# Self-attention and feed-forward in one program, the first up products between the last tiles

## The reference

```python
x = x + xattn(layernorm(x), ctx_768, ...)
# self-attention: 16 heads of 32, 32 rows in a sequence
qkv = layernorm(x) @ w_attn
scores = q @ k.T / sqrt(32) + causal - log1p(softplus(decay) * log1p(dist))
x = x + (softmax(scores) @ v) @ w_proj
# feed-forward: 512 -> 2048 -> 512
h = round8(layernorm(x) @ w1 + b1)         # to multiples of 2^-8
h = round8(piecewise_linear_gelu(h))       # 33 breakpoints on [-4, 4]
x = x + round8(h @ w2 + b2)
```

## Time and profile before

| | us |
|---|---|
| median of 3 runs | 1637.65 (1637.59 to 1638.66) |
| profiled execution: first to last instruction | 1631.5 |
| median run less that span | 6.15 |
| TensorE busy | 1582.6 |
| self-attention's first product to its last | 992.94 to 1247.58 |
| feed-forward's first product | 1249.76 |
| granted TensorE clock over the span | 0.993 of 2.4 GHz |

### The profile page before, as it was taken

The page is one execution under the profiler, slowest core; times in us unless marked ns, Lnnn a source line. Parts: engine busy times, 40 slices in busy tenths (PEclk is TensorE's granted clock), DMA queues, the critical chain, the costliest instruction groups (busy, mean ns, idle before and its releaser), DMA issues. The chain is left out here.

```text
span 1631.5 us, 30117 instructions
## 1 busy us (share of the span) xinstructions
PE 1582.6 (97%) x11126; PEld 1382.6 (85%) x11126; DVE 1229.8 (75%) x2404; ACT 1033.8 (63%) x2050; POOL 771.8 (47%) x722
## 2 busy tenths in 40 slices
PE   7999999999999999999999999999998999999998
PEld 5878899998999999899999778988886777878886
DVE  5548888877887888878887784666666988788886
ACT  3347777777777777777786422445446766666665
POOL 2316546364554546555453241334435545555554
PEclk9999999999999999999999999999998999999999
DMA  7983434444343443534353862011132221010010
GB/s 232 276 244 95 135 91 113 121 112 134 90 123 111 108 134 95 140 95 110 114 144 83 290 220 72 21 60 62 64 111 79 71 71 53 26 52 20 7 52 26
DMA packets 173826, 173.63 MB, mean 106 GB/s; under 512 B 80944, under 2 KB 138352, under 8 KB 173680
## 3 DMA queue, kind: packets, MB, share of 16 engines
q1 hardware_dynamic: 173680, 171.71, 36.2%
HBM read 133.91 MB, written 37.75 MB: 105 GB/s over the span
## 5 line engine op out<-in xcount | busy, mean ns | idle before, releaser
L75 PE MATMUL p_bank_score<-p_ctxt,p_qo 128*128 128x256 f32 x2304 | 304.5, 286 | 1.0 <-ACT p_probs L998 0.6
L75 PEld LDWEIGHTS p_bank_score<-p_ctxt,p_qo 128*128 128x128 f32 x2304 | 288.1, 191 | 6.1 <-issue 2.4
L75 PE MATMUL p_bank_mix<-p_probt,p_ctx 128*128 128x512 f32 x1152 | 292.1, 398 | 0.5
L75 PEld LDWEIGHTS p_bank_mix<-p_probt,p_ctx 128*128 128x128 f32 x1152 | 207.5, 189 | 41.8 <-issue 3.8
L2017 PE MATMUL p_bank_down<-p_w,p_ht 128*128 128x512 f32 x768 | 188.2, 393 | 7.0 <-DVE p_raw L2091 4.9
L1990 POOL TENSOR_TENSOR p_pieces<-p_pieces 128x512 f32<-128x512 f32 x64 | 112.3, 1755 | 159.2 <-ACT p_pieces L2057 159.2
L1201 DVE SCALAR_TENSOR_TENSOR p_qo<-p_bank_mix,p_odd,p_qo 128x512 fp32r<-128x512 f32 x192 | 143.8, 749 | 57.2 <-ACT p_qo L1012 49.5
L704 POOL TENSOR_TENSOR p_ctx<-p_ctx_in,p_ctx 128x768 fp32r<-128x768 f32 x64 | 118.3, 1849 | 131.6 <-ACT p_ctx L987 131.2
L2017 PEld LDWEIGHTS p_bank_down<-p_w,p_ht 128*128 128x128 f32 x768 | 143.8, 188 | 42.1 <-DVE p_raw L2091 6.5
L1012 ACT ACTIVATE p_qo<-p_bank_mix,p_odd 128x512 fp32r<-128x512 f32 x192 | 132.2, 689 | 67.8 <-PE p_bank_mix L75 67.4
L998 ACT ACTIVATE p_probs<-p_bank_score,p_small 128x257 f32<-128x257 f32 x256 | 121.3, 475 | 58.9 <-DVE p_small L1182 54.4
(11 more groups left out here) (276 smaller groups left out, 3631.9 us busy)
## 6 DMA issues: line engine op xcount, KB each, us to landing
p_blocks_in<-in_ctx_dram SPq DMA_DIRECT2D x256, 96.0 KB, 2.4
p_ctx_in<-in_ctx_dram SPq DMA_DIRECT2D x64, 384.0 KB, 3.1
q<-p_ctx SPq DMA_DIRECT2D x64, 256.0 KB, 3.6
p_odd_in<-in_ctx_dram SPq DMA_DIRECT2D x64, 192.0 KB, 3.5
p_x<-in_x_dram SPq DMA_DIRECT2D x32, 256.0 KB, 4.2
p_quad<-q SPq DMA_DIRECT2D x32, 256.0 KB, 3.8
p_probt<-q SPq DMA_DIRECT2D x32, 256.0 KB, 4.1
p_o_in<-o SPq DMA_DIRECT2D x8, 1024.0 KB, 7.1
```

Source lines behind the costliest of these rows:

```text
L75: made = e.matmul(out, lhsT, rhs, start=n == 0, stop=n == last)
```

## The change

The two blocks become one. Each engine runs its list of self-attention and then that of the feed-forward with no meeting between them, and parts of the feed-forward's lists (`following`) are called from within self-attention's.

- TensorE: up products 0 to 4 lie between the scores, mixes and projections of the last two tiles; up 5 precedes the first down product.
- The activation chain of product 0, the rounding of products 1 to 3 and the Abs and Relu of product 0 lie in self-attention's lists. What waits for them stays in order.
- The next stage's first four row tiles are turned in t = 8 to 11, as a second turn of each tile, and no longer in t = 12 to 15. Rows are scaled in place in four buffers, and a row's buffer is loaded again once it is turned.
- The late pieces: four in t = 14 and four in t = 15 (two on VectorE and two on GpSimd in each), the last four in n = 1 to 4 of the feed-forward.
- The last four projections use the turning bank. LayerNorm's moments for the feed-forward are prepared in three parts: 0 to 3, 4 to 11 (now in t = 14), 12 to 15 (n = 17 to 20).
- The bias is loaded at the start of self-attention, behind four row loads where there were three ahead of the decay's.

```diff
 def sync(e, following):
+    for p in range(4):
+        load_row(p)
     e.dma_start(dec[:], decay_raw[None, :].to_broadcast([P, HS])).then_inc(decay_in, DMA)
...
+    e.wait_ge(norm.steps, 14)
+    following.load_bias(e)
...
+        if t == LAST:
+            late_is_split(e, 2)
+            for k in range(2):
+                following.load_block(e, k)
 LAST = NT - 2 ; PAIRED = NT - 8
-LATE_EVEN = {NT - 2: ((0,), ()), NT - 1: ((2,), ()), NT: ((4, 6), (8, 10))}
-LATE_ODD = {NT - 2: ((), (1,)), NT - 1: ((), (3,)), NT: ((5, 7), (9, 11))}
+LATE_HI = {LAST: range(4), LAST + 1: range(4, 8)}
+LATE_EVEN = {LAST: (0, 2), LAST + 1: (4, 6)}
+LATE_ODD = {LAST: (1, 3), LAST + 1: (5, 7)}
 def tensor(e, following):
+    def turn_own(i):
+        j = i - PAIRED - 4
+        if j > 0:
+            e.wait_ge(after.norm.lo, j)
+        norm.turn(e, i)
+    def turn_next(j):
+        e.wait_ge(norm.lo, PAIRED + 4 + j + 1)
+        after.norm.turn(e, j)
+    for t in range(LAST):
+        scores(t)
+        project_slice("q", t + 2, 0, queried)
+        project_slice("k", t + 2, C, keyed)
+        if t >= 1:
+            mix(t - 1)
+        if t + 4 < NT:
+            turn_own(t + 4)
+        if t >= 2:
+            project(t - 2)
+        if PAIRED <= t < PAIRED + after.early:
+            turn_next(t - PAIRED)
+        project_values(t + 2)
+    scores(LAST)
+    project(LAST - 2)
+    following.up(e, 0)
+    mix(LAST - 1)
+    following.up(e, 1)
+    scores(LAST + 1)
+    project(LAST - 1)
+    mix(LAST)
+    following.up(e, 2)
+    following.up(e, 3)
+    mix(LAST + 1)
+    project(LAST)
+    following.up(e, 4)
+    project(LAST + 1)
 def scalar(e, following):        # t = 15, then behind the loop
+    if t == NT - 1:
+        following.fold(e, 0)      # Gelu's table, Abs, Relu
+following.gelus(e, 0)            # behind the cuts of tile 15
 def vector(e, following):        # in t
     e.wait_ge(scored, NB * (t + 1))   # mask, max
+    if t == NT - 1:
+        following.rounded_up(e, 0)
...                              # sum, reciprocal
+    if t == NT - 1:
+        following.rounded_up(e, 1)
...                              # transposition
+    if t == LAST:
+        after.norm.finish(e, 1)
+    if t + 4 < NT:
+        norm.low(e, t + 4, *ahead.place(t + 4))
+    if t >= 2:
+        sums(t - 2)
+    if PAIRED <= t < PAIRED + after.early:
+        after.norm.low(e, t - PAIRED, after.zt, (t - PAIRED) * P)
+    for k in late_blocks(LATE_EVEN, t):
+        low_late_even(e, k)
+# behind the loop
+following.rounded_up(e, 2)
+following.snap(e, 0)
+following.rest_of(e, 0)
+following.rounded_up(e, 3)
+sums(LAST)
+following.combine(e, 0)
+sums(LAST + 1)
 # feed-forward
 def tensor(e):
-    for n in range(NT + LAG):
-        if n < NT:
-            up(n)
-        if n >= LAG:
-            down(n - LAG)
+    for n in range(LAG, NT + LAG):
+        if n == LAG:
+            up(e, n + 1)
+        if n > LAG + 1 and n < NT:
+            up(e, n)
+        down(n - LAG)
 def scalar(e):
+    for n in range(1, NT + LAG):      # fold(n), gelus(n), high_block(n), high half of h
+        if n <= 4:
+            attention.late_high(e, 7 + n)
+        if n == KF + 2:
+            norm.root(e, 2)
 def vector(e):
+    for n in range(1, NT + LAG):      # from n = 4 on rounded_up(n)
+        if n == KF + 1:
+            norm.guard(e, 2)
+        if n == KF + 4:
+            norm.finish(e, 2)
+        if n in (2, 4):
+            attention.low_late_even(e, 6 + n)
```

More of the change, by code:

```diff
@@ L1396, in self_attention @@
         y_stats = room.sb("y_stats", [P, 6])
-        norm.banks = after.norm.banks = room.banks("turn", 1)
-        after.norm.z = norm.z
+        turn = room.banks("turn", 1)
+        norm.banks = turn
         mm = room.banks("mm", 3)
@@ L1444, in bank_of @@
         def bank_of(kind, n):
-            return mm[use_at[kind, n] % 3]
+            return mm[use_at[kind, n] % 3] if (kind, n) in use_at else turn[0]
         def bank_is_free(e, kind, n):
+            if (kind, n) not in use_at:
+                if n == LAST - 2:
+                    e.wait_ge(after.norm.lo, after.early)
+                else:
+                    e.wait_ge(added, n)
+                return
             at = use_at[kind, n]
@@ L1478, in sync @@
                 load_y(i)
+            e.wait_ge(norm.steps, 14)
+            following.load_bias(e)
             for t in range(NT):
-                if t + 7 < NT + after.early:
-                    load_x(t + 7)
+                for p in range(4, len(rows)):
+                    if row_step(p - 4) == t:
+                        load_row(p)
                 if t + 2 in WEIGHTS:
@@ L1803, in vector @@
             e.wait_ge(made, 7)
[L1804 removed]
+            for t in range(NT):
                 if t == SEEN:
@@ L1862, in feed_forward, with __init__ @@
+class FeedForward:
+    def __init__(self, begun, programs):
+        (self.load_bias, self.load_block, self.make_constants, self.up, self.fold, self.gelus, self.rounded_up,
+         self.snap, self.rest_of, self.combine) = begun
+        self.programs = programs
+def feed_forward(nc, ahead, attention, spare, w1, x2_dram, w_1, b_1, w_2, b_2, out_rows):
     G = 512
@@ new lines, in make_constants, with up @@
+        def make_constants(e):
+            e.memset(plus, MAGIC).then_inc(consts, 1)
+            e.memset(minus, -MAGIC).then_inc(consts, 1)
+            e.memset(last, LAST).then_inc(consts, 1)
+            e.memset(base, -SNAP - LAST).then_inc(consts, 1)
+            e.memset(quarter, STEP - SNAP - LAST).then_inc(consts, 1)
+        def up(e, n):
+            g, f = divmod(n, KF)
+            zt = zts[g % 2]
+            if f == 0:
+                e.wait_ge(norm.lo, NR * (g + 1))
+            if n == 0:
+                e.wait_ge(ahead.w_lo, KT)
+            if g == 0 and f >= KT and f % KT == 0:
+                attention.late_is_split(e, f // KT)
+            if n >= 3:
+                e.wait_ge(rounded, n - 2)
+            else:
+                attention.bank_is_done(e, n)
+            accumulate(e, b_up[n % 3], [t for k in range(KT) for t in three(
+                lambda s, k=k: first_weights(s, k, f),
+                lambda s, k=k: zt[:, s, k, :])]).then_inc(upped, 1)
@@ new lines, in fold @@
+        def fold(e, n):
+            m, a, w = (x[n % SETS] for x in (m_, a_, w_))
+            if n == 0:
+                e.wait_ge(consts, 5)
+                e.activation(scratch, quarter, ACT.Gelu).then_inc(ready, 1)
+            e.wait_ge(rounded, n + 1)
+            if n >= SETS:
+                e.wait_ge(downed, NR * (n - SETS + 1))
+            e.activation(a[:], m[:], ACT.Abs, bias=minus).then_inc(absed, 1)
+            e.wait_ge(absed, n + 1)
+            e.activation(w[:], a[:], ACT.Relu, bias=last, scale=-1.0).then_inc(left, 1)
```

479 lines of the change are left out of this document (236 added, 243 removed).

## The result

The changed kernel takes 1644.74 us in the median of five runs (1642.48 to 1645.9), the kernel before on the same chip 1637.65 (1635.88 to 1641.58). The ratio is 1.0047, with a 95% interval of 1.0033 to 1.0062: 5.4 to 10.2 us more. I had forecast 1639.6 and "no change" as the likeliest. The time lies 0.3 under the upper end of my range (1633.5 to 1645.0) and outside the sum's own, 1636.0 to 1641.9, and the sign is slower.

What follows compares the result with a forecast made beforehand. TensorE, busy 97% of the span, was taken as the bound. Terms 0.82 + 6.12 + 0.43 - 5.4 = +2.0 us on 1637.65 gave 1639.6; range 1633.5 to 1645.0, the sum's own 1636.0 to 1641.9.

Steps and rivals of the forecast that it cites:

- Behind it both orders are the same, and the lead stays as the chain's: After product 3 of the feed-forward: its 5.4 us of earliness against the kernel before lasts to the end.
- -5.4 for the end: From the scores of tile 14 on: product 3's low half of h at 60.7 instead of 66.14, 5.4 us earlier.
- the 17.9 from product 0 to 3: Low half of h, product 0 to product 3: 15.92 us before, 17.9 with late pieces 8 and 10 on VectorE.
- product 0's low half at 42.8: Start of the low half of h for product 0, 42.8 us after the scores of tile 14; before, 50.22.
- late pieces 8 and 10: Two weight pieces on VectorE between products 0 and 3: 0.65 to 1.64 us each, taken as 1.0.
- The third moment part: LayerNorm work in feed-forward group 1: costs nothing, as low halves are ready some 5 us early; without that, up to 4.
- The second turn: Tiles 8 to 11: it waits for VectorE's low half, stalling TensorE 1.53 us four times, +6.12; lowest price 1.39 each.
- The fourth row load ahead of the decay's: Start of self-attention: the extra load's issue on SyncE delays the decay by 0.43 us, at least 0.
- (1): Rival, faster: the second turn doesn't hold TensorE, only occupancies remain; -4.1, 1633.5 us; chance 0.17.
- (2): Rival, slower: TensorE's clock falls at the stalls in tiles 8 to 11; one +3.7, four +8.8 us; chance 0.2.
- (3): Rival, slower end: product 0's activation chain starts another 2 us later than 42.8; +4.0, 1641.6 us; chance 0.2.
- product 3's low half at 60 to 62: Sign in the feed-forward: prediction wrong if product 3's low half of h isn't 60 to 62 us after tile 14's scores.

Runs made afterwards that it cites:

- run 11: Run 10's kernel with late weight pieces 8 to 11 moved out of the steps of products 2 to 5 into engines' idle time: 1631.29 us, ratio 0.9968.
- run 10: Changed kernel with the edits of run 3, run 5, run 7 and run 9, and the decay's load ahead of the fourth row load: 1636.12 us, ratio 0.9991.
- run 9: Changed kernel with VectorE's snap and rest of product 1 ahead of combining product 0 and the sums of tile 15: ratio 1.0029 to the kernel before.
- run 5: Changed kernel with the third moment part on GpSimd except its reciprocal: ratio 1.0040 to the kernel before.
- run 6: Changed kernel with the low halves of late pieces 8 and 10 on GpSimd in place of VectorE: ratio 1.0059 to the kernel before.
- run 1: Kernel before with 64 bytes of padding ahead of the feed-forward's row, activation and h buffers: ratio 1.0003.
- run 2: Changed kernel with the gap ahead of the feed-forward's buffers raised from 80 to 96 words: ratio 1.0036 to the kernel before.
- run 7: Changed kernel with 192 bytes more ahead of the feed-forward's buffers (gap of 128 words): ratio 1.0047 to the kernel before.
- run 3: Changed kernel with the second turn of tiles 8 to 11 behind the value products: ratio 1.0006 to the kernel before.
- run 8: Changed kernel with the edits of run 3, run 5, run 6 and run 7, and the decay's load ahead of the fourth row load: 1637.76 us, ratio 1.0003.
- run 4: Kernel before with the feed-forward's PSUM banks in the changed kernel's order (turning bank first, then up, then down): ratio 0.9997.

## Why the prediction was wrong

**The failed step** is "Behind it both orders are the same, and the lead stays as the chain's", with the size of the lead that went into it. The sum booked -5.4 for the end; the end gave -0.42. The first step to fail is the one right ahead of it, the 17.9 from product 0 to 3. The missing 5.0 are four leaks, in the order in which they come:

- *The step to product 3*, 1.4. The start of the chain was right: product 0's low half at 42.8 forecast, 42.55 measured (1269.89 less 1227.34). But from there to product 3 I took 17.9, "late pieces 8 and 10 ... at 0.65 to 1.64 each; I take 1.0", and it was 19.54: 1.36 of the lead, after the 0.25 that product 0 came sooner. The 2.0 booked for the pieces was about right, as all four together cost 2.1 (run 11 against run 10), VectorE's own two at 1.77 and 1.79. What I put at nothing is the snap of product 1: I had the sums of tile 15 stand ahead of it and charged them to no step, and they cost 1.0 (run 9). The other 0.5 is in the step to product 1, which even in run 11 takes 5.39 for 4.85; no run says why. A further 0.2 goes by product 4.
- *The third moment part*, 1.2, booked as "nothing" because low halves were ready 5 us before their down products. That slack is TensorE's, within the group. VectorE has none: it is the chain across the next group boundary, so the 1.2 from product 16 to 19 (3.77 to 2.61) were lost for good, 1.0 of them in the one step that run 5 shortened. My "up to 4" for a missing cover was too high.
- *The place of the buffers*, in no term: 1.3 us of the last group, where TensorE sets the end (the profiles of runs 5, 6 and 9; 1.5 and 1.6 in those of runs 1 and 2, none in run 7's). The profile of before couldn't show it; the diff, which re-ordered the allocations, could have raised the question.
- *A fall of the clock in this one profile*, 1.0. From product 48 to 63 the lead falls by 2.3, where runs 5, 6 and 9, with the same buffers, lose 1.3. In this profile and in run 3's, which loses 2.2, the granted clock fell beside product 34, in those of runs 5, 6 and 9 beside product 18. The same 8 us of the changed kernel and of run 9, columns as in the earlier trace rows, the clock 0.79 and 1.00:

```profile
1466.00:1474.00 8.00, 6.20 (x19) 4.31 (x19) 6.86 (x11) 4.12 (x6) 0.77 (x2) 0.79 0.49 175
1466.00:1474.00 8.00, 7.58 (x32) 5.53 (x31) 6.73 (x12) 4.93 (x8) 1.45 (x1) 1.00 0.61 217
```

  TensorE is later from there on: product 57's down product starts 7.9 after its low half has ended, in runs 5, 6 and 9 7.3. Run 7 has that fall too and loses nothing, so it costs only together with the slower pace. That the fall is the cause rests on two profiles against three; no run was made for it.

So 5.4 less 1.4, 0.2, 1.2, 1.3 and 1.0 leaves 0.3, and 0.42 was measured; 0.1 came back between product 19 and 48. One more chance is in the number that I started from: product 0's 50.22 of the kernel before is 49.4 and 49.3 in runs 1 and 4, so 0.9 of every lead here is that profile's.

**Right, by its numbers.** The second turn waits each time. Counted as I counted it, from 2.89 after the projection's start, the wait is 1.44 where I had 1.53 (1190.35 and 1194.68; the profile's own idle time, which begins at the modelled end, is 1.29, under my floor of 1.39). Tiles 8 to 11 came to +7.77 for the forecast 7.76 (run 3 splits it into 6.0 of wait and 1.76 of turns); that it fits to the hundredth is luck. Tiles 12 and 13 gave back 0.80 for 0.82. The first down product came at 44.34 for "43 to 44", the wait before mix 14 was 1.97 for 2.4, and the two late pieces of tile 14 took 3.41 for 3.28. The Trainium skill, SBUF — State Buffer, section "Who interferes with whom", would have made that 3.9, by the prediction's estimate; what it says of who blocks fits all the same: a piece that started beside a running GpSimd operation took 1.77 (changed kernel, 1274.31), and one that started 0.02 ahead of it 0.66, while GpSimd's took 1.66 for 1.16 (run 11, 1253.01).

**A term too small.** The fourth row load ahead of the decay's: 0.43 booked as its issue. The wait for the decay grew from 3.55 to 4.5, and the stage to the scores of tile 0 by 0.93. All seven profiles with the fourth row load ahead wait 4.1 to 5.1; with the decay's load ahead of it again it was 3.6 to 3.9 (runs 8, 10 and 11), and 3.3 to 4.0 with the kernel before's own order.

**The rivals.** (1), that the turn doesn't hold TensorE, is excluded by the waits. (2), a fall of the clock at those waits, didn't happen: the clock is 1.00, and tiles 8 to 11 take 68.01 to 68.05 in all six profiles that keep the paired turn. (3) had the right sign with the wrong place, and is too small, +4.0 where the median rose by 7.1: the chain starts in time and then falls behind. That the time lies inside the range is luck: its upper end was made of two falls of the clock in tiles 8 to 11, and none came. My test "product 3's low half at 60 to 62" just failed at 62.10, and that was the first sign.

## What to carry to other kernels

A lead is worth what is left of it at the next place where its engine is the bound. Follow the engine that carries it through every stage to the end, and charge each operation that the change puts on that engine, however short and however well covered for the others. Work that must go near a chain through several engines belongs in a gap in which all of them wait, ahead of the chain (run 11: 5.2 us under the kernel before to run 10's 1.5 by the ratios, 4.4 to 3.1 by the profiles), not between its steps on whichever engine looks idle. And a wait for a buffer can be hidden by putting independent work between the two uses (run 3: 6.0 us for one moved line).

## What the runs showed of the hardware

The pace of a dense stretch of products depends on where its two SBUF operands lie: 227 ns a matmul of 512 columns with h and the turned rows at 128 modulo 256 bytes (two places of h, 162944 and 157056), as the other operand, and 231 to 233 ns at 192 and at 0 (the kernel before and run 7; the changed kernel, run 1 and run 2). PSUM's order changes nothing (run 4). It is the pair that counts: the same rows at 128 took 234 ns with the quarter of w1 at 224. That equal places modulo 256 are what makes a pair fast is only my reading, and it isn't clean: rows and weights both at 224 took 231 in the third group of the kernel before. The Trainium skill, TensorE: Matmul & The Clock Gate, section "Step-by-step: what each phase is for", says that loading the next weights takes no SBUF bandwidth from the running matmul. From that sentence alone I should not have expected the two places to matter to each other, and here they do by 3%; by which mechanism, no run shows.
